# A two-layer graph network on one core: who adds x and h2, and what GpSimd's queue holds

## What is computed

```python
h = maximum(layernorm(x), 0)
# layer 1
score = sum(h[src] * h[dst], -1)
a = softmax of score over the edges of one dst
agg = segment_sum((h @ W_conv + b_conv)[src] * a, dst)
out = agg + relu(h @ W_res + b_res)
x2 = x + batchnorm(out)            # mean and variance over all nodes
# layer 2
h2 = maximum(layernorm(x2), 0)
m = gelu(gelu([h2[src], h2[dst], edge_attr] @ W_m1 + b_m1) @ W_m2 + b_m2)
boxes = segment_sum(m, dst)
c = gelu(gelu([h2, boxes] @ W_c1 + b_c1) @ W_c2 + b_c2)
return x2 + h2 + c
```

## Time and profile before

| | us |
|---|---|
| median of 3 runs | 1828.24 |
| the profiled execution | 1824.53 |
| its span on the core | 1822.7 |

### The profile page before, as it was taken

How to read it: one execution, slowest core, us unless ns; L and a number is a source line. 1 busy time by engine, 2 the same in 40 slices (tenths; PEclk the granted TensorE clock), 3 DMA queues, 4 the chain that set the end, 5 groups by cost and what they waited for, 6 DMA issues and landing times.

```text
span 1822.7 us, 22166 instructions
## 1 busy us (share of the span) xinstructions
PE 1313.4 (72%) x6521; PEld 875.2 (48%) x6521; DVE 1351.0 (74%) x2253; ACT 927.7 (51%) x1840; POOL 1233.3 (68%) x1062
## 2 busy tenths in 40 slices
PE   3441756765737475275898898888885998899994
PEld 1231545554526354164666666566664443444431
DVE  7832776798649387187979998688854998799972
ACT  4511533453325242163666776476651776577772
POOL 7774664677765747500868887667867878887675
PEclk8755776786778676587888997798875999899996
DMA  7751764654435332125344554555555764566620
GB/s 216 258 177 34 285 231 155 209 200 141 117 95 166 100 114 90 36 99 220 110 160 157 194 185 161 163 176 189 174 160 127 183 162 121 133 146 156 139 49 16
DMA packets 132615, 273.56 MB, mean 150 GB/s; under 512 B 30404, under 2 KB 47658, under 8 KB 132496
## 3 DMA queue, kind: packets, MB, share of 16 engines
q1 hardware_dynamic: 76004, 187.38, 30.8%
q0 software_dynamic: 39360, 43.42, 12.0%
q10 hardware_dynamic: 17132, 41.35, 6.1%
HBM read 151.68 MB, written 121.80 MB: 150 GB/s over the span
## 4 chain that ended last, share of the span: by engine, by line
PE 29%; issue 24%; POOL 18%; another core or an unknown queue 10%; DVE 10%; ACT 5%; DMA 3%; ACTq 0%; SPq 0%; POOLq 0%; DVEq 0%
POOL agg_rows L609 11%; PE banks L1503 4%; POOL out L609 4%; PE banks L1387 3%; PE banks L1579 2%; DVE stat L772 2%; PE banks L1372 2%; PE banks L1577 2%; PE banks L1493 2%; PE banks L1586 2%; DVE stat L764 2%; PE banks L1553 2%; PE banks L1593 2%; POOL agg_ring L605 2%
## 5 line engine op out<-in xcount | busy, mean ns | idle before, releaser
L605 POOL DMA_INDIRECT part<-in_x,edge_idx x192 | 212.1, 1104 | 124.1 <-DVE part L774 66.3
L605 POOL DMA_INDIRECT agg_ring<-agg_rows,edge_idx x196 | 233.5, 1191 | 84.8 <-issue 56.4
L609 POOL DMA_INDIRECT agg_rows<-agg,put_first x196 | 232.2, 1185 | 58.0 <-issue 57.6
L609 POOL DMA_INDIRECT out<-agg,put_last x196 | 215.5, 1100 | 67.3 <-issue 59.8
L1503 PEld LDWEIGHTS banks<-packed,cT 97*128 97x128 f32 (+1 forms) x1568 | 216.3, 223 | 45.1 <-issue 45.1
L1372 PE MATMUL banks<-ident,xc 128*128 128x128 f32 (+1 forms) x784 | 137.6, 326 | 136.6 <-issue 76.4
L1503 PE MATMUL banks<-packed,cT 97*128 97x64 f32 (+1 forms) x1568 | 224.4, 309 | 0.0
L1099 ACT ACTIVATE hT<-banks 128x512 f32<-128x512 f32 (+1 forms) x98 | 55.5, 594 | 324.0 <-remote 165.4
L1387 PE MATMUL banks<-hT,packed 128*128 128x512 f32 (+1 forms) x196 | 132.2, 810 | 78.9 <-issue 54.3
L1372 PEld LDWEIGHTS banks<-ident,xc 128*128 128x128 f32 (+1 forms) x784 | 113.9, 177 | 147.5 <-issue 100.6
L1493 PE MATMUL banks<-hT,packed 64*96 64x512 f32 (+1 forms) x392 | 127.7, 730 | 59.6 <-ACT cT L1216 45.9
(11 more groups left out here) (166 smaller groups left out, 3195.2 us busy)
## 6 DMA issues: line engine op xcount, KB each, us to landing
xt<-in_x SPq DMA_DIRECT2D x84, 512.0 KB
r_rows<-rT ACTq DMA_DIRECT2D x48, 512.0 KB
agg_rows<-rb SPq DMA_DIRECT2D x48, 512.0 KB
out<-xt SPq DMA_DIRECT2D x36, 512.0 KB
edge_r<-rr ACTq DMA_DIRECT2D x48, 256.0 KB
rT<-r_rows SPq DMA_DIRECT2D x24, 512.0 KB
part<-r_rows SPq DMA_DIRECT2D x24, 512.0 KB
rr<-edge_r SPq DMA_DIRECT2D x48, 256.0 KB
```

What stands on the lines that cost most here:

```text
L605: A.indirect_dma_start(to, None, table[:, :], bass.IndirectOffsetOnAxis(ap=idx, axis=0), bounds_check=limit, oob_is_err=False).then_inc(si ...
L609: A.indirect_dma_start(table[:, :], bass.IndirectOffsetOnAxis(ap=idx, axis=0), rows_of, None, bounds_check=limit, oob_is_err=False).then_i ...
```

## The change

VectorE adds h2 in all steps, two adds in a row ahead of the second step's x2. Its `scale_r` gets a third operation, which adds x of the edges; SyncE loads that x into four buffers, the two dedicated ones of the gather ring and the two halves of one gout buffer. GpSimd thus only issues indirect DMAs: in the node pass all puts and then all gathers of agg, 5/3 groups a step in place of 4/3 where SyncE's stores are placed, and in the edge pass the final scatters alone. Gathers no longer check their indices, and the last group is gathered and scattered with all 128 partitions; its agg is set to 0 at the start, and its padded indices are 0 for gathers and out of the table for scatters.

```diff
+        x_in = x_ring[0:4]
...
-        B_y = stage("h2_added_on_gpsimd")
         B_yv = stage("h2_added_on_vector")
...
-        C_x = slots("edge_x_added", 4)
+        C_x = slots("edge_x_loaded", 4)
...
-        C_ra = stage("edge_r_scaled", 2)
+        C_ra = stage("edge_r_scaled", 3)
...
         def agg_groups(s):
-            return PUTS_AHEAD + 4 * (s + 1) // 3
+            return PUTS_AHEAD + 5 * (s + 1) // 3

         def h2_added(eng, s):
             if s >= 0:
-                (B_yv if s % 2 else B_y).done(eng, s // 2)
+                B_yv.done(eng, s)
...
+            def load_edge_x(g):
+                C_ra.done(sp, g - 4)
+                if g in (2, 3):
+                    sp.wait_ge(B_fin.sem, B_fin.after(S - 1))
+                p = edges_of(g)
+                sp.dma_start(x_in[g % 4][0:p, :], edge_x[g][0:p, :]).then_inc(C_x.of(g), 16)
...
                     for g in range(6):
+                        if g < 2:
+                            load_edge_x(g)
                         if g < 4:
                             load_attr(g)
                             load_agg(g)
...
                 if i == 0:
                     for g in range(2, 4):
+                        load_edge_x(g)
+                    for g in range(2, 4):
                         load_prev(g)
-                for g, do in ((a + 4, load_agg), (a + 6, load_edges), (a + 5, load_agg), (a + 7, load_edges),
-                              (a + 4, load_prev), (a + 5, load_prev)):
+                for g, do in ((a + 4, load_agg), (a + 4, load_edge_x), (a + 6, load_edges), (a + 5, load_agg),
+                              (a + 5, load_edge_x), (a + 7, load_edges), (a + 4, load_prev), (a + 5, load_prev)):
...
             def gather(to, table, idx, signal):
-                A.indirect_dma_start(to, None, table[:, :], bass.IndirectOffsetOnAxis(ap=idx, axis=0),
-                                     bounds_check=limit, oob_is_err=False).then_inc(signal, 16)
+                A.indirect_dma_start(to, None, table[:, :], bass.IndirectOffsetOnAxis(ap=idx, axis=0)).then_inc(signal, 16)
...
                 for j in range(EJ):
-                    scatter(agg_rows, idx_of(put_first, g, j, p), agg_of(g, p)[:, j * D:(j + 1) * D], G_p.of(n))
+                    scatter(agg_rows, idx_of(put_first, g, j, P), agg_of(g, P)[:, j * D:(j + 1) * D], G_p.of(n))
...
-            def add_x(g):
-                p = edges_of(g)
-                C_ra.done(pool, g)
-                A.dma_start(rr[g % 6][0:p, :], edge_x[g][0:p, :], accum_op=ALU.add).then_inc(C_x.of(g), 16)
-
-            def add_h2(s):
-                p = nodes_of(s)
-                pool.wait_ge(B_h.sem, B_h.after(s))
-                here = xb[s % XB][0:p, :]
-                A.tensor_tensor(here, here, xc[s % CS][0:p, :], ALU.add).then_inc(B_y.sem, 1)
...
             for s in range(S):
-                if s % 2 == 0:
-                    add_h2(s)
                 for n in range(agg_groups(s - 1), agg_groups(s)):
...
-            ahead = agg_groups(S - 1) - G
+            ahead = min(G, agg_groups(S - 1) - G)
...
             for g in range(G):
-                add_x(g)
                 if is_group(g + ahead):
                     gather_agg(g + ahead)
...
+            V.memset(agg_of(G - 1, P), 0.0)
...
-                if is_step(a - 1):
-                    add_h2_here(a - 1)
+                for s in (a - 2, a - 1):
+                    if is_step(s):
+                        add_h2_here(s)
...
                 V.tensor_tensor(here, here, cols(bn[0:p, 0, :], ER), ALU.mult).then_inc(C_ra.sem, 1)
+                dve.wait_ge(C_x.of(g), C_x.after(g))
+                dve.wait_ge(C_ra.sem, C_ra.after(g, 2))
+                V.tensor_tensor(rr[g % 6][0:p, :], rr[g % 6][0:p, :], x_in[g % 4][0:p, :], ALU.add).then_inc(C_ra.sem, 1)
...
-                pe.wait_ge(C_x.of(g), C_x.after(g))
+                pe.wait_ge(C_ra.sem, C_ra.after(g))
                 T.matmul(to, ident[0:p, 0:p], rr[g % 6][0:p, :], start=True, stop=False)
```

More of the change, by code:

```diff
@@ L620, in gather_x @@
                         c = (2 * j + k) * D
-                        gather(x_ring[n % GS][0:p, c:c + D], x, idx_of(idx, g, j, p), G_x.of(n))
+                        gather(x_ring[n % GS][:, c:c + D], x, idx_of(idx, g, j, P), G_x.of(n))
             def put_agg(n):
                 g = group_of(n)
-                p = edges_of(g)
                 G_p.done(pool, n - 4)
@@ L636, in gather_agg @@
                 for j in range(EJ):
-                    gather(agg_ring[g % RS][0:p, j * D:(j + 1) * D], agg_rows, idx_of(src_idx, g, j, p), G_a.of(g))
-            def add_x(g):
-                p = edges_of(g)
-                C_ra.done(pool, g)
-                A.dma_start(rr[g % 6][0:p, :], edge_x[g][0:p, :], accum_op=ALU.add).then_inc(C_x.of(g), 16)
-            def add_h2(s):
-                p = nodes_of(s)
-                pool.wait_ge(B_h.sem, B_h.after(s))
-                here = xb[s % XB][0:p, :]
-                A.tensor_tensor(here, here, xc[s % CS][0:p, :], ALU.add).then_inc(B_y.sem, 1)
+                    gather(agg_ring[g % RS][:, j * D:(j + 1) * D], agg_rows, idx_of(src_idx, g, j, P), G_a.of(g))
             def put_final(g):
-                p = edges_of(g)
                 C_put.done(pool, g - 4)
@@ L655, in put_final @@
                 for j in range(EJ):
-                    scatter(out, idx_of(put_last, g, j, p), agg_of(g, p)[:, j * D:(j + 1) * D], C_put.of(g))
+                    scatter(out, idx_of(put_last, g, j, P), agg_of(g, P)[:, j * D:(j + 1) * D], C_put.of(g))
             for n in range(G):
```

## The result

Measured beside each other, the kernel before takes 1830.72 us (median of 4 runs, 1814.08 to 1838.15) and the changed kernel **2082.57 us** (4 runs, 2070.09 to 2088.9): ratio 1.138, 95% interval 1.129 to 1.148. The change made it slower by 252 us; the prediction of 1780, its range and its sign were wrong.

The account below looks back on a forecast made before the run. No engine is full in the first pass, where TensorE's results sometimes come late while GpSimd issues; VectorE paces the node pass, PE and VectorE the edge pass. 1824.5 - 26 - 18 - 8 + 27 - 11.5 - 5 - 2.4 gives 1780 us, range 1755 to 1880.

Parts of the forecast that it names:

- Step (1): First pass: without GpSimd's wait for the first h2, puts go on and the long stall goes, -26 us.
- TensorE stands until the puts run out: Rival, chance 0.3: TensorE late until GpSimd's puts end, first pass near 960 (+95), total 1895 or 1845 us.
- Step (6): Unchecked gathers, all passes: no change taken; ends 0.1 us each, 39 us over the first pass, gain or loss.
- gathers become cheaper: Rival, chance 0.05: unchecked gathers save 0.1 us each, half of it kept, total 1760 us or less.
- Step (2): Node pass: both h2 adds on VectorE and gathers at 5/3 groups a step, -18 us; ends -38 and 0.
- Step (3): Between node and edge pass: SyncE's loads of x in advance shorten TensorE's wait, -8 us; ends -13 and 0.
- Step (4): Edge pass: two more VectorE adds a pair cost +27 us, the thin stretch 1500 to 1592 goes, -11.5 us.
- Step (5): Full last group: quicker DMAs at the first eight gathers and last four scatters, -5 and -2.4 us.

Follow-up runs that it names:

- e16: Kernel before with the node pass's part alone (GpSimd neither waits for h2 nor adds, 5/3 groups a step): 1954.03 us, 1.054 times the kernel before.
- e11: Changed kernel with the pause restored (GpSimd waits for the first h2, adds nothing): 2131.23 us.
- e13: Changed kernel with the bounds check put back on its gathers, where the kernel before takes 1825.11 us: 1996.78 us, ratio 1.089.
- e12: Changed kernel in which GpSimd waits for each group of puts that follows the gathers to land: 2038.03 us.
- e2: Kernel before with unchecked gathers and nothing else changed: 1581.9 us, ratio 0.985 to the kernel before.
- e14: Kernel before with unchecked gathers and nothing else changed, on a chip where the kernel before takes 1825.11 us: 1927.04 us, ratio 1.057.
- e5: Kernel before with the node pass's part alone (both h2 adds on VectorE, 5/3 groups a step): 1613.3 us, ratio 1.003.
- after_again: Changed kernel, unaltered, run again for its trace on another chip: 1600.6 us, ratio 0.995 to the kernel before.
- before_again: Kernel before, unaltered, run again for its trace on another chip: 1606.7 us.
- e6: Kernel before with the edge pass's part alone (x of edges loaded by SyncE, added by VectorE): 1618.47 us, ratio 1.009.
- e4: Kernel before with a full last group (128 indices in every gather and scatter): 1599.24 us, ratio 0.994.
- e15: Kernel before with GpSimd waiting after every second group of x gathers until it has landed: 1744.15 us, ratio 0.938.
- e8: Changed kernel with GpSimd waiting after every second group of gathers or puts in the first two passes: 1785.78 us, ratio 1.110.
- e7: Kernel before with unchecked gathers and a full last group together: 1568.3 us, ratio 0.976.

## Why the prediction was wrong, step by step

**Step (1), the pause, failed.** It was taken at -26 us. On a late chip it is worth roughly +90 to +125: with the whole node pass's part the first pass ends at 978 instead of 854 (e16), and the pause alone, put back into the changed kernel, takes off 91 (e11). The rival "TensorE stands until the puts run out" had the place, nearly the mechanism and, for this part, nearly the size: +95, first pass near 960, "a wait of over 80 us on VectorE ending some 3 us after GpSimd stops". Measured: 978 and 982 us, waits of 91 and 96 us; the end came 16 us after GpSimd's stop in e16 and already during the last puts in e13. Its own total of 1895 us was 188 us too low all the same, since it too priced the unchecked gathers at nothing. And what it shares with the rest of the prediction, that the lateness lasts until GpSimd pauses, is too strong: two stops of the changed kernel ended with GpSimd still issuing. Two arguments kept its chance at 0.3, and both were weak. "In the node and edge passes GpSimd issued as densely with no such stall": in e11 and e12 the node pass has stalls once the puts lie in it without GpSimd's adds, which broke its run in the kernel before; this reading fits, but no run put only the adds back. "Long stalls entered at random would hardly allow" runs within 1%: they are not random in sum; on such chips no run of the kernel before was under 1801 us, where the others never took over 1614.

**Step (6), unchecked gathers, failed.** It was taken at 0 with ends of 39 us. On an on-time chip it is -27 us (e2, 1.5%), inside the ends, and the rival "gathers become cheaper" was right there. On a late chip it is +102 us (e14, 1927.04 against 1825.11): 74 in the first pass, 18 in the node pass. A price of the instruction by itself could not show that: the gathers got shorter here too (0.95 instead of 1.00 us), and the loss is waiting. The sum and the rival priced the two steps as if they were independent of the stalls.

**Step (2), the node pass, failed in size on both sorts.** Predicted -18. On an on-time chip the part alone costs 16 us (473 to 489), with SyncE's ordered waits as its visible cause; with cheaper gathers after_again has 475, -18 became +2. The pace of 20.3 us a pair that the prediction worked out for the gathers is what e5 has on average (489 / 24 = 20.4): I averaged it away over ten pairs at 18.8 and wrote 19.9 for the other fourteen without a reason. What the prediction expected of adds and gathers side by side came out in part: with GpSimd's adds gone the final adds to the xt buffers take 1218 ns in the mean (e5) instead of 1333 (before_again), but the gathers got no longer beside more adds of VectorE, 1228 against 1253 ns. On a late chip the pass lost 35 us in the whole change.

**Step (3)**, between the passes, -8: the whole change has 42 us where before_again has 41, so nothing came of it. e6 has 34, but so have e2, e4 and e5, which leave the loads of x alone; this stretch changes by 7 us for other reasons. What moved is who waits: TensorE's wait for the x DMAs, 28.5 us in all, fell to 3.0 in after_again, and VectorE waits 9.6 us there for the x of group 2 or 3, which the prediction had named and not priced.

**Step (4), the edge pass, held as a sum.** +27 - 11.5 = +15.5 was predicted; measured are +15 in the first comparison (370 to 385), +15 between before_again and after_again and +11 in e6. No run separates the two terms. The new adds of after_again from 1150 to 1525 us, against the 0.71 us of the prediction:

```profile
L996 DVE TENSOR_TENSOR rr<-rr,gout 128x512 f32<-128x512 f32 x24 | 16.6, 693 | 12.0 <-DMA gout<-edge_x 9.6
L996 DVE TENSOR_TENSOR rr<-rr,x_ring 128x512 f32<-128x512 f32 x22 | 15.2, 693 | 2.3
```

**Step (5)**, -7.4: e4 gives 1599.24 for 1608.96, -10 us, 8 of them in the first pass, where 5 were predicted. Held.

In sum, on the on-time chips the stages changed by -24, +2, +1, +15 and -4 = -10 us, a ratio of 0.995 where the prediction had 0.974. The parts measured alone (e2, e4, e5, e6) sum to -22 us, and the whole gives -8.5, so some 14 us of their interplay stay unexplained. On the late chips the two mis-sized steps (1) and (6) are worth about 200 us together.

## What to carry to other kernels

Look at what ends a stall before removing a wait: if it ended when one engine stopped, that engine's pause may be a resource. The price of taking it away is then not zero, and can be as long as the run that follows (a run of 112 us was estimated here, and e16's first pass lost 125). Breaks in GpSimd's run of indirect DMAs, one after every 16 gathers, gained 80 us of first pass on one sort of chip (e15) and cost 68 on the other (e8, which had them in the puts too), so such a choice must be measured on the chips that it is meant for. And a trace with an unexplained "remote" wait of tens of us is worth a second trace on another chip before its parts are priced.

## What the runs showed of the hardware

The same program, the kernel before, took 1603 to 1614 us on two chips and 1801 to 1916 us on three others and in the first measurement. Two of these chips were met twice (15 and 10 by their numbers on record), each both times as the same sort. That the chip makes the difference, and not what else ran beside it, is inferred from this. The indirect DMAs take the same time on both (a scatter alone 0.97 us, a checked gather 1.00, an unchecked one 0.94, medians of the first pass); the difference is waiting, 206 of 218 us in the first pass for the kernel before and 426 of 488 for the changed one. On the late chips TensorE at times advances by one instruction per 1.40 us while GpSimd issues indirect DMAs each 1.27 us or so, and ScalarE has waited up to 104 us and VectorE up to 96 us for its results. Where GpSimd stops, VectorE's long stop ends 6 to 16 us later (after, e11, e14, e16); some stops end while it still issues; and breaks of GpSimd make them shorter (e15). On the on-time chips a stream just as dense does no such thing. TensorE's granted clock was 0.50, the lower of its two levels (1.2 GHz), from 800 to 950 us, after a stretch in which PE was busy for 13.5 of 50 us. The clock alone cannot be the lateness: the matmuls recorded in e11's picture take 0.37 us, and the rest of each 1.40 us is waiting.

The Trainium skill, SBUF — State Buffer, "Who interferes with whom", names the port pair that VectorE shares with GpSimd as the only source of contention between engines; by it TensorE could not be held up by GpSimd. The rows of e11 and the result of e15 show that here it is. Through what, no run shows.

Open is what differs between the chips, what it is that TensorE waits for (its records say "issue": nothing that the profile shows), and why unchecked gathers make the lateness worse. Their edit changes both the length of the DMA (0.94 for 1.00 us) and whether a register write has to stand ahead of each group, and no run separated the two. Nor was there a run with e7's edits and e15's breaks together, or of e7 on a late chip.
